# Attention scores on Trainium2: in each step VectorE takes the maxima of the first pass in front of the decay product instead of behind it

## The reference, cut to what matters

```python
std_logits = jnp.einsum('bhqd,bhkd->bhqk', q, k) * scale
incidence = jnp.einsum('bqhp,bkhp->bhqk', read_lines, J_write)
weights = decays[:, None, None] ** diffs_pos[None] * past[None]
bias = incidence * weights[None] * bias_scale[None, :, None, None]
logits = jnp.where(causal_mask[None, None], -jnp.inf, std_logits + bias)
attn = jax.nn.softmax(logits, axis=-1)
out = jnp.einsum('bhqk,bhkd->bqhd', attn, v)
```

## Time and profile before

| what | value |
|---|---|
| time, median of 3 runs | 1121.7 us (1119.39 to 1123.53) |
| profiled execution, first to last instruction | 1169.6 us |
| PE busy (share of the span) | 988.7 us (85%) |
| DVE busy | 895.8 us (77%) |
| POOL busy | 807.0 us (69%) |
| ACT busy | 718.4 us (61%) |
| additions of L853 | 256, the first starts at 90.1 us, the last at 838.7 us |

### The profile page before, as it was taken

One profiled execution on the slowest core, in us unless ns is written; L12 is line 12 of the kernel. 1 busy time (PEld: TensorE's weight loads), 2 busy tenths in 40 slices (PEclk: granted clock), 3 DMA queues, 4 the chain that ended last, 5 costly groups with the idle time before them and its releaser, 6 DMA issues. The chain is left out here.

```text
span 1169.6 us, 31325 instructions
## 1 busy us (share of the span) xinstructions
PE 988.7 (85%) x9473; PEld 782.6 (67%) x9473; DVE 895.8 (77%) x2317; ACT 718.4 (61%) x1612; POOL 807.0 (69%) x1346
## 2 busy tenths in 40 slices
PE   2448999999999999999999999988627888988857
PEld 2337777777777777777777777767416776776742
DVE  6668899899998999899989999899554554545436
ACT  3426777777777777787787778774524444544420
POOL 6456768888888888888888888873353555555544
PEclk9989999999999999999999999999858999999989
DMA  8356465646555565655565656563013422222239
GB/s 232 112 146 185 141 173 156 187 145 178 164 173 166 165 177 157 182 152 172 160 186 148 185 155 184 155 182 108 29 46 76 150 77 74 72 76 76 69 109 352
DMA packets 226195, 170.47 MB, mean 146 GB/s; under 512 B 61872, under 2 KB 188272, under 8 KB 225904
## 3 DMA queue, kind: packets, MB, share of 16 engines
q1 hardware_dynamic: 212384, 143.22, 42.9%
q0 software_dynamic: 8448, 17.45, 4.7%
q10 hardware_dynamic: 5200, 7.79, 1.9%
HBM read 90.81 MB, written 76.78 MB: 143 GB/s over the span
## 5 line engine op out<-in xcount | busy, mean ns | idle before, releaser
L1101 ACT ACTIVATE PT<-sc 128x768 f32<-128x768 f32 x256 | 206.8, 808 | 184.1 <-DVE sc L853 177.1
L870 DVE TENSOR_REDUCE peak<-pre 128x6 f32<-128x768 f32 x256 | 243.4, 951 | 41.1 <-PE pre L707 40.9
L1587 POOL DMA_INDIRECT yab<-y_out,xt x136 | 131.4, 966 | 126.7 <-DVE y_out L1534 92.1
L853 DVE TENSOR_TENSOR sc<-sc,tt 128x512 f32<-128x512 f32 x256 | 176.7, 690 | 20.2 <-PE sc L694 19.3
L902 DVE TENSOR_TENSOR tt<-inc,decay 128x512 f32<-128x512 f32 x256 | 174.6, 682 | 1.1 <-PE inc L681 0.4
L1309 POOL DMA_INDIRECT xg<-stage,slot_i x128 | 130.8, 1022 | 63.3 <-issue 43.8
L692 PE MATMUL sc<-queries,KT 128*128 128x256 bf16 x512 | 141.4, 276 | 16.6 <-ACT PT L1101 12.8
L707 PE MATMUL pre<-causal,identb 128*128 128x256 bf16 x512 | 141.7, 277 | 0.0
L706 PE MATMUL pre<-KT,queries 120*128 120x256 bf16 x512 | 140.5, 274 | 0.0
L694 PE MATMUL sc<-identb,causal 128*128 128x256 bf16 x512 | 139.8, 273 | 0.0
L705 PE MATMUL pre<-KT,queries 120*128 120x128 bf16 x512 | 114.6, 224 | 12.7 <-DVE peak L870 7.2
(11 more groups left out here) (272 smaller groups left out, 2784.3 us busy)
## 6 DMA issues: line engine op xcount, KB each, us to landing
KT<-kq_rows SPq DMA_DIRECT2D x128, 240.0 KB
queries<-kq_rows SPq DMA_DIRECT2D x128, 168.0 KB
kq_rows<-dim_part SPq DMA_DIRECT2D x64, 192.0 KB, 2.4
kq_rows<-line_part SPq DMA_DIRECT2D x64, 144.0 KB
QI<-kq_rows SPq DMA_DIRECT2D x128, 72.0 KB
xt<-xg SPq DMA_DIRECT2D x136, 65.0 KB
kq_rows<-dim_part SPq DMA_DIRECT2D x64, 128.0 KB, 2.2
kq_rows<-line_part SPq DMA_DIRECT2D x64, 96.0 KB
```

The source lines that it names most:

```text
L853: nc.vector.tensor_tensor(diag, diag, tt[p % 2][:], ALU.add).then_inc(added.sem, 1)
L870: nc.vector.reduce_max(peak[half][:, i:i + 2, 0:3], pre[:, :, 0:3 * P].rearrange("p n (g k) -> p n g k", g=3), AX.X)\
L1101: nc.scalar.activation(PT[p % 4][:], sc[:, :, 0:3 * P], ACT.Exp).then_inc(exped.sem, 1)
L1587: nc.gpsimd.indirect_dma_start(yab, bass.IndirectOffsetOnAxis(xt[r][:, D:D + 1].bitcast(i32), 0), y_out[r % 8][:], None).then_inc(y_sent[r ...
```

## The change

In the body of DVE's step the two calls of `weigh` move from in front of the maximum of `pre` to behind it. Nothing is added or removed, and the lists of the other engines are the same as before. In the changed kernel the maximum is on line L866, its small second maximum on L871; `weigh` stays on L902 and the addition on L853.

```diff
                         bank_copies(b, p)
-                        if p < 7 and live(b):
-                            weigh(b, p + 1)
-                        if p == 7 and live(b) and live(b + 1):
-                            weigh(b + 1, 0)
                         if b < 0 and p == 1 and live(b + 3):
...
                             if pp % 4 == 3:
                                 wait(dve, maxed, pb, 4 * half + 4)
                                 nc.vector.reduce_max(peak[half][:, :, 3], peak[half][:, :, 1:3], AX.X).then_inc(peaked.sem, 1)
+                        if p < 7 and live(b):
+                            weigh(b, p + 1)
+                        if p == 7 and live(b) and live(b + 1):
+                            weigh(b + 1, 0)
                         extras(b, par, p)
```

## The result

The changed kernel takes **1203.5 us** (1202.93 to 1208.35 in four runs) against 1121.1 us: slower, by a ratio of 1.0744 with a 95% interval of 1.072 to 1.0767, or 82.4 us. The forecast was 1198 us in a range from 1172 to 1230.

What follows compares the result with a forecast made beforehand. Attention was taken as a ring through PE, DVE and ACT; the change closes a DVE-PE ring whose eight turns sum to 26.24 us a batch against 23.72. 31 x 2.52 = +78 us, taken as 76 on 1121.7: 1198 us, range 1172 to 1230.

Steps and rivals of the forecast that it cites:

- turn: Time from the start of one maximum of `pre` to the next; bare 2.59 us, eight turns sum to 26.24 us a batch.
- the ring: Closed loop of DVE and PE without overlap: maximum, `weigh`, incidences, first pass, next maximum; 2.59 us a bare turn.
- The hand-over from `weigh` to PE: From `weigh`'s end on DVE to the start of PE's incidences: 0.05 us, bounds nothing and 0.16.
- My discount for the excess of the first span: First profile's span lay 47.9 us above the runs' median, so +78 us was taken as 75 to 78, used as 76.
- `attnT` at 0.28: Two PE transposes between incidences and first pass in the turn from 2 to 3, priced like `back`: 0.28 us.
- the extras: DVE's further work in a step, 0.71 us in step 4; in the other steps said to fit beside PE's part.
- The turn from 4 to 5: Set by DVE's own work: 1.74 + 0.71 + 0.60 = 3.05 us, more than the ring's 2.79.
- The turn from 5 to 6: PE's `back` waits for DVE's `heads_norm`, now behind `weigh`: 2.08 + 1.04 us, together 3.12.
- The signs in the trace: PE waits for `weigh` in nearly each step; the maximum waits for the first pass in nearly all 248, some 0.3 us or more.
- A wait of PE for ACT: Sign of being wrong: ACT or POOL shows up as what PE or DVE wait for.
- The rival of more waits: Waits for ACT or POOL of 0.35 us in two steps of each batch: +22 us, about 1222 us; chance 0.17.
- The clock: TensorE's clock left at full, 1.00 mid-attention; rival of a partly lowered clock: about 1230 us, chance 0.04.

Runs made afterwards that it cites:

- the second profile of the kernel before: The kernel before, unchanged, profiled a second time: 1120.9 us in one run, a span of 1118.8 us.
- the added length: Changed kernel plus a DVE reduction of 0.41 us in each step with a second pass: 1278.3 us between maximum and `weigh`, 1217.6 us just before the next addition.
- the ring is opened on PE: Changed kernel, but PE issues the incidences of a step behind the first pass instead of in front of it: 1161.9 us.
- with the product in the ring: Changed kernel plus a DVE product of two SBUF tiles between maximum and `weigh` in each step with a second pass: 1425.9 us.

## Why the prediction was right, point by point

- **The chain through maximum, `weigh` and PE's waits sets the batch: shown.** Forecast and measured turns, beside those of the second profile of the kernel before:

| turn | before | forecast | after |
|---|---|---|---|
| 0 to 1 | 3.57 | 3.90 | 3.91 |
| 1 to 2 | 2.57 | 2.59 | 2.61 |
| 2 to 3 | 2.56 | 3.12 | 3.04 |
| 3 to 4 | 3.20 | 3.46 | 3.50 |
| 4 to 5 | 3.07 | 3.05 | 2.98 |
| 5 to 6 | 2.64 | 3.12 | 3.12 |
| 6 to 7 | 3.12 | 3.54 | 3.55 |
| 7 to 0 | 2.88 | 3.46 | 3.50 |
| batch | 23.61 | 26.24 | 26.21 |

That the added length counts in full inside the ring and hardly outside it (74.8 and 14.0 us), and that half of the loss comes back when the ring is opened on PE, stands behind it. The errors of the turns, up to 0.08 us, cancel to 0.03 in the sum. No run gave `inc` a second tile, which would open the ring without changing the order of either list.

- **The hand-over from `weigh` to PE**, taken at 0.05 from a bank job, is 0.06 (407.14 to 407.20).
- **The 5.5 us by which the time lies above the forecast** come from the base and from the scaling, not from the ring. I had taken 23.72 us a batch before the change from the first profile; the second has 23.61, and (26.21 - 23.61) x 31 = 80.6 us in place of 78. The attention as a whole grew by 81.3, the runs by 82.4. My discount for the excess of the first span (76 for 78) was wrong too: most of the excess lay in the experts.
- **`attnT` at 0.28**, borrowed from `back`, was too much: from the start of the incidences to the first pass are 0.44 us (410.04 to 410.48) where I had 0.52, and the turn from 2 to 3 came out 0.08 shorter.
- **The turn from 4 to 5** came out 0.07 shorter for another reason. I took the extras from the end of the small maximum, in front of which nothing overlaps. Behind `weigh` the first of them starts 0.08 before `weigh` has ended, and the sum lacked that overlap.
- **The turn from 5 to 6** goes as forecast: `heads_norm` (L1004) ends at 419.74, `back` starts at 419.79.

```profile
418.70 0.28 PE L692 MATMUL sc<-queries,KT 128*128 128x256 bf16 x1 [0.40 <-ACT PT L1101]
...
419.45 0.29 DVE L1004 TENSOR_TENSOR attn<-bank,rden 128x128 f32<-128x128 f32 x1
...
419.79 0.44 PE L792 MATMUL bank<-ident,h2T 128*128 128x128 f32 x2
```

- **The signs in the trace held in part.** I had asked for PE's wait for `weigh` in nearly each step, and for the wait of the maximum in nearly all of 248 steps. They show in four of eight steps (six with the small ones) and in six of eight. Where PE's wait is small or missing (turns from 2, 3, 5 and 6), PE's own list or its wait for the exponential is about as long; where the maximum doesn't wait (steps 2 and 5), DVE's own list is. For the turns from 2, 4 and 5 my table had said as much, for the others it hadn't. A wait of PE for ACT was to be a sign of being wrong. There is one, the 0.40 us above, but in that turn PE waits for `heads_norm` afterwards, so it doesn't set the length.
- **The rival of more waits** (1222) didn't happen. ACT's wait for the addition grew from 131.7 to 174.4 us, but ACT isn't in the ring, and the turn from 0 to 1, where `lines` could have waited for ACT, took 3.91 us for a forecast 3.90.
- **The clock** stayed at 1.00 from 400 to 495 us though PE waited 0.65 to 0.67 us for `weigh` in four of the eight steps of each batch (the columns are those of the earlier trace rows):

```profile
400.00:495.00 95.00, 82.99 (x916) 64.70 (x913) 77.46 (x183) 67.06 (x136) 73.50 (x136) 1.00 0.52 155
```

What the Trainium skill ("TensorE: Matmul & The Clock Gate", section "A second HAM failure mode: psum-queue depth-cycling") says of frequent small idle times between matmul groups didn't show at these gaps.
- **One sentence of the forecast wasn't right as a picture of the whole.** It priced the extras behind `weigh` at nothing except in two turns. In the changed kernel that holds, since the ring hides them. With the ring opened they are late, and some 40 of the 82 us stay, in the turns from 0, 3 and 5. How much of that is `heads_norm`, how much the later addition and how much `hT` wasn't separated by a run.

## What to carry to other kernels

When two engines feed each other through tiles that exist once, write the waits down as a closed ring and add up its turn, from a start to the next start. An instruction moved behind one that waits on the same partner can close such a ring, even if every engine has air and no work is added. Look first at the order in which the partner delivers: here a decay product ahead of the maximum cost nothing, since it filled the time in which the maximum had nothing to read.

## What the runs showed of the hardware that wasn't expected

A VectorE product with both operands in SBUF took 3.06 us instead of 0.42 when GpSimd ran two-operand instructions on SBUF tiles at the same time. The product started at 491.07, during `line_rest`, and ended at 494.13, in the last of four `outer`: it waited through several of GpSimd's instructions. `line_rest` and the first three `outer` kept their length (1.64 and 0.72 us). The fourth took 0.90 us, by the mean of all batches, where it takes 0.74 in the changed kernel. A VectorE reduction with one SBUF operand at the same place took 0.41 us always (0.407 to 0.414), though it too lay beside such instructions of GpSimd in more than 100 of 256 cases. The Trainium skill states the rule in "SBUF — State Buffer", section "Who interferes with whom": a VectorE instruction with two SBUF inputs contends with a GpSimd instruction that reads SBUF, a reduction on this chip never does. By that rule, the traces agree. `weigh` reads one operand from PSUM, and its longest was 0.692 us in this kernel and in the changed one.

In the same kernel, with the product in the ring, PE waited up to 3.6 us for `weigh` and was busy 435 of 600 us, and the granted clock was 0.93 on average. The second row is a stretch behind one of these waits, which ended at 494.79:

```profile
200.00:800.00 600.00, 435.37 (x4410) 333.87 (x4408) 487.42 (x1038) 324.47 (x649) 360.38 (x653) 0.93 0.39 116
...
496.50:499.50 3.00, 3.00 (x28) 2.02 (x21) 1.74 (x4) 2.30 (x7) 1.77 (x2) 0.50 0.10 33
```

So it reached its lower level there, once in each batch, and between 200 and 800 us of the changed kernel it never did.
